# Row maxima of causal attention from the exponentials' operands, on the whole array, in three buffers

## What is computed

```python
scores = jnp.einsum('bhqd,bhkd->bhqk', q, k) * D ** (-0.5)
scores = jnp.where(causal, scores, -jnp.inf)
weights = jax.nn.softmax(scores, axis=-1)     # needs each query's maximum first
out = jnp.einsum('bhqk,bhkd->bhqd', weights, v)
```

## Time and profile before

| | |
|---|---|
| runs | 719.22 us median (716.24, 719.22, 719.84) |
| the profiled execution's own time | 713.31 us |
| its span, first to last instruction | 711.5 us |
| mean granted TensorE clock | 0.949 of full speed |
| TensorE (PE) busy | 616.2 us, 87% |
| VectorE (DVE) busy | 504.4 us, 71% |
| ScalarE (ACT) busy | 455.0 us, 64% |
| GpSimd (POOL) busy | 259.0 us, 36% |
| DMA | 52.09 MB in 33323 packets |

### The profile page before, as it was taken

One profiled execution on the slowest core, in us unless ns is written; L12 is line 12 of the kernel. 1 busy time (PEld: TensorE's weight loads), 2 busy tenths in 40 slices (PEclk: granted clock), 3 DMA queues, 4 the chain that ended last, 5 costly groups with the idle time before them and its releaser, 6 DMA issues.

```text
span 711.5 us, 14086 instructions
## 1 busy us (share of the span) xinstructions
PE 616.2 (87%) x4988; PEld 293.0 (41%) x5052; DVE 504.4 (71%) x825; ACT 455.0 (64%) x908; POOL 259.0 (36%) x459
## 2 busy tenths in 40 slices
PE   0687399499988999999999999899999999999983
PEld 0455033245453555444352354432333333346632
DVE  7967588375775546888978978599988898843222
ACT  0463156266646688778766676687777777766781
POOL 5665021314300211687111106791132221116883
PEclk9788579799998999999999999999999999999997
DMA  5057431300551300306230444063331330200002
GB/s 175 0 180 156 125 121 40 68 1 31 139 156 41 71 28 4 95 23 189 75 91 18 81 116 126 2 180 125 71 85 33 80 67 18 53 2 1 1 0 60
DMA packets 33323, 52.09 MB, mean 73 GB/s; under 512 B 5832, under 2 KB 23912, under 8 KB 30696
## 3 DMA queue, kind: packets, MB, share of 16 engines
q1 hardware_dynamic: 31960, 50.74, 26.8%
q10 hardware_dynamic: 1296, 0.46, 0.2%
HBM read 37.29 MB, written 13.63 MB: 72 GB/s over the span
## 4 chain that ended last, share of the span: by engine, by line
PE 56%; DVE 13%; POOL 12%; ACT 6%; issue 6%; DMA 4%; SPq 2%; another core or an unknown queue 0%; POOLq 0%; ACTq 0%; DVEq 0%
PE ps L1319 52%; DVE maxes L1302 5%; ACT probs L1034 3%; DVE sine L1156 2%; POOL gate L550 2%; DMA qop<-shiftT 2%; SPq L736 2%; POOL probs L862 2%; PE ps L1534 1%; DMA F<-in_w 1%; POOL xn L550 1%; PE ps L1373 1%; POOL gate L907 1%; POOL gate L908 1%; POOL x L897 1%
## 5 line engine op out<-in xcount | busy, mean ns | idle before, releaser
L1302 DVE TENSOR_REDUCE maxes<-ps 128x2 f32<-128x1024 f32 (+2 forms) x288 | 338.6, 1220 | 91.1 <-PE ps L1319 89.5
L1034 ACT ACTIVATE probs<-ps 128x512 f32<-128x512 f32 x576 | 305.3, 605 | 110.0 <-PE ps L1319 68.5
L1319 PE MATMUL ps<-qop,kop 128*128 128x512 bf16 (+3 forms) x704 | 163.8, 327 | 22.4 <-DMA qop<-shiftT 9.3
L862 POOL TENSOR_SCALAR_AFFINE_SELECT probs<-probs 128x512 f32<-128x512 f32 (+1 forms) x160 | 83.8, 546 | 249.1 <-ACT probs L1034 249.1
L1319 PE MATMUL ps<-probs,vals 128*9 128x512 f32 (+3 forms) x1536 | 150.1, 493 | 4.9 <-POOL probs L862 3.1
L1319 PE MATMUL ps<-kmx,qmx 32*128 32x128 bf16 (+2 forms) x1280 | 101.9, 269 | 20.6 <-DMA qop<-shiftH 8.9
L1319 PEld LDWEIGHTS ps<-qop,kop 128*128 128x128 bf16 x768 | 60.2, 99 | 110.7 <-ACT probs L1034 50.0
L1319 PEld LDWEIGHTS ps<-kmx,qmx 32*128 32x128 bf16 x1280 | 38.1, 93 | 118.4 <-issue 66.4
L1319 PE MATMUL ps<-F 128*128 128x128 f32 (+2 forms) x640 | 76.9, 283 | 5.4 <-DMA F<-in_w 3.9
L1319 PEld LDWEIGHTS ps<-F 128*128 128x128 f32 (+2 forms) x640 | 69.2, 181 | 20.2 <-issue 16.3
L1319 PEld LDWEIGHTS ps<-probs,vals 128*9 128x9 f32 x1536 | 29.7, 90 | 60.5 <-issue 43.8
(11 more groups left out here) (158 smaller groups left out, 643.4 us busy)
## 6 DMA issues: line engine op xcount, KB each, us to landing
qop<-q_thirds SPq DMA_DIRECT2D x48, 192.0 KB
kop<-k_thirds SPq DMA_DIRECT2D x48, 192.0 KB
qmx<-q_thirds SPq DMA_DIRECT2D x16, 256.0 KB
kmx<-k_thirds SPq DMA_DIRECT2D x16, 256.0 KB
F<-in_w SPq DMA_DIRECT2D x16, 256.0 KB, 5.1
q_thirds<-third SPq DMA_DIRECT2D x8, 384.0 KB, 4.4
k_thirds<-third SPq DMA_DIRECT2D x8, 384.0 KB, 3.8
q_thirds<-third SPq DMA_DIRECT2D x8, 256.0 KB, 3.3
```

Source lines behind the costliest of these rows:

```text
L862: last = pool.affine_select(where, where, [[0, number], [1, P]], ALU.is_ge, 0.0, base=0, channel_multiplier=-1)
L1034: act.activation(probs[:, u % RING, :], bank(at), ACT.Exp, scale=SCALE).then_inc(s_cells_read, 1)
L1302: dve.tensor_reduce(dst, src, AX.X, ALU.max).then_inc(s_units_read[pair // 2], 1)
L1319: return pe.matmul(out_, lhsT, rhs, start=first, stop=last)
```

## The change

The operands for the maxima, their loads and the DRAM planes that only they used are gone. A max product now reads rows 0 to 125 of `qop` and `kop`, the whole height of the array, one head after the other. The shift's rows move to 126 and 127. `qop` and `kop` get three buffers, so a load waits for the group three back. For groups 0 and 8 the load comes in two halves, each after its own half of the store, with its own semaphore; their max units are cut so that the first six need only half 0 (20 units instead of 18). The shift's DMAs are issued by ACT, right behind its copy, not by SP. The planner gets new costs and a new `MORE` table, and no longer counts max units as a tiling of their own.

```diff
-KR = TERMS * D
+KR = P - 2
-QUERY_COPIES = ((0, 0, 2), (2, 0, 3))
-KEY_COPIES = ((0, 0, 3), (3, 0, 2), (5, 1, 1), (6, 0, 1))
+QUERY_COPIES = ((0, 0, 3),)
+KEY_COPIES = ((0, 0, 3), (3, 0, 2))
+DEEP = 3
...
+HALVES = [[(2, 0, 256), (3, 0, 256)], DIAGONALS[0], [(1, 0, 128), (3, 256, 128)], [(5, 512, 128), (7, 768, 128)]] + LATER_ROWS
...
-SHAPE = {"max": "rows", "pv": "columns", "eo": "halves"}
-STAY = {"whole": 27.0, "rows": 57.0, "columns": 20.0, "halves": 10.0, None: 0.0}
+SHAPE = {"pv": "columns", "eo": "halves"}
+STAY = {"whole": 2.0, "rows": 160.0, "columns": 29.0, "halves": 10.0, None: 0.0}
...
 MORE = {
-    "add": (47, -2), "attT": (-5, -48), "colsum": 13, "comb": 49, "count": -1, "ct": 2, "diag": -80, "disp": 17, "emb": 4,
...
+    "add": (160, 45), "attT": (55, -88), "colsum": 157, "comb": -18, "count": 160, "ct": -11, "diag": 118, "disp": -120,
...
-        masks = 2 * COLUMN * BANK + TILING + 0.1 if arg[1] // 2 in DIAGONAL else 0.0
-        return COLUMN * BANK + masks, "D", (("DVE", 1.2),)
+        pieces = pattern(arg[0])[arg[1] // 2]
+        masks = 2 * COLUMN * BANK if pieces in DIAGONALS else 0.0
+        return 2 * COLUMN * sum(w for _, _, w in pieces) + masks, "D", (("DVE", 0.1 + 0.0022 * sum(w for _, _, w in pieces)),)
...
     if kind == "ldexp":
-        return [("ldmax", n)] + ([("exp", n - 2, NU - 1)] if n >= 2 else [])
+        return [("store", n // NG, 2 * (n // GB % 2) + half) for half in ((0, 1) if c == 2 else (c,))] + (
+            [("exp", n - DEEP, NU - 1)] if n >= DEEP else [])
...
-        qmx = sb("qmx", [P, 2, T], BF16)
-        kmx = sb("kmx", [P, 2, T], BF16)
-        qop = sb("qop", [P, 2, HG, T], BF16)
-        kop = sb("kop", [P, 2, HG, T], BF16)
+        qop = sb("qop", [P, DEEP, HG, T], BF16)
+        kop = sb("kop", [P, DEEP, HG, T], BF16)
...
-                elif kind == "ldmax":
...
+                elif kind == "ldexp":
+                    n, part = arg
+                    r, L, b, heads = n % DEEP, n // NG, n // GB % 2, slice(n % GB * HG, n % GB * HG + HG)
+                    for half in (0, 1) if part == 2 else (part,):
                         sp.wait_ge(s_stored[half], STORES * (2 * L + b + 1))
+                    if n >= DEEP:
+                        sp.wait_ge(s_cells_full, CELL["exp", n - DEEP, NU - 1] + 1)
...
+                        sp.dma_start(qop[rows_i, r, :, some], q_rows).then_inc(s_loaded[0 if part == 2 else part][r], 16)
+                        sp.dma_start(kop[rows_i, r, :, some], k_rows[D * i:D * i + 3 * D]
+                                     ).then_inc(s_loaded[1 if part == 2 else part][r], 16)
-                elif kind == "shift":
-                    n, part = arg
-                    sp.wait_ge(s_cells_read, CELL[what] + 1)
...
@@ ACT, shift
+                        act.wait_ge(s_cells_read, CELL[what] + 1)
+                        for k in range(2):
+                            act.dma_start(qop[KR + k:KR + k + 1, r, :, :], shiftT[HG * TB * k:HG * TB * k + HG * TB, :]
+                                          ).then_inc(s_shift_in[k][r], 16)
...
@@ PE, max
-                    pe.wait_ge(s_mload[r], 32 * (n // 2 + 1))
+                    for half in (0, 1) if n not in SPLIT or u >= units(n, 0) else (0,):
+                        pe.wait_ge(s_loaded[half][r], 48 * arrivals(n))
...
-                            rows_h = slice(MR * h, MR * h + MR)
-                            last = mm(bank(pair + k)[:, c:c + w], qmx[rows_h, r, P * i:P * i + P],
-                                      kmx[rows_h, r, k0:k0 + w], not diagonal, not diagonal or c + w == BANK)
+                            last = mm(bank(pair + k)[:, c:c + w], qop[0:KR, r, h, P * i:P * i + P],
+                                      kop[0:KR, r, h, k0:k0 + w], not diagonal, not diagonal or c + w == BANK)
```

More of the change, by code:

```diff
@@ L101, in parts, with pattern, units, arrivals @@
     return (0, 1) if n in SPLIT else (2,)
+def pattern(n):
+    return HALVES if n in SPLIT else PATTERN
+def units(n, part=2):
+    return 6 if part == 0 else 2 * len(pattern(n))
+def arrivals(n):
+    return n // DEEP + 1 + sum(k <= n and k % DEEP == n % DEEP for k in SPLIT)
 def of_part(kind, n, part):
@@ L131 @@
 WINDOW, KEEP, REGAIN = 3.4133, 0.48, 0.8
-WEIGHT = {"max": 0.25, "shift": 0.25}
+WEIGHT = {"shift": 0.25}
 ENGINES = ("PE", "ACT", "DVE", "POOL", "SP")
+OF_GROUPS = ("max", "exp", "pv", "top", "shift", "halve", "pvout", "out", "mask", "ldmax", "ldexp")
 MORE = {
-    "add": (47, -2), "attT": (-5, -48), "colsum": 13, "comb": 49, "count": -1, "ct": 2, "diag": -80, "disp": 17, "emb": 4,
[L137 to L144, removed]
@@ new lines @@
+    "add": (160, 45), "attT": (55, -88), "colsum": 157, "comb": -18, "count": 160, "ct": -11, "diag": 118, "disp": -120,
+    "emb": -119, "embT": 58, "embstat": 5, "eo": 158, "es": -35, "exp": (48, -75), "halve": (-99, -77), "heads": (-45, 129),
+    "hid": 48, "hid1": -104, "high": (-102, 103, -120), "ldexp": (138, 28), "ldf1": -82, "ldw": -11, "ldwA": -31,
+    "ldwB": 110, "left": (-51, 75, -50), "lg": -28, "limit": 93, "ln": 122, "lnroot": 12, "lnstat": 56, "logit": -17,
+    "low": (-27, -38, 130), "lt": 145, "mask": (106, 150), "max": (33, -61), "middle": (142, -37, 26), "mix": -85,
@@ new lines @@
+    "norm": (16, 131, -3), "offs": -40, "out": (37, -45), "proj": (-31, -98), "pv": (-94, -114), "pvout": (76, 134),
+    "qk": (54, 133, 65), "rT": 151, "rden": (-99, -97), "res": -120, "root": (-120, 48), "routes": 20, "rs": 45,
+    "shift": (-77, -45), "silu": (137, -21), "slot": 76, "soft": 96, "stat": (-120, -47, -117), "store": (-103, -45, -98),
+    "sum": (125, 13, 119), "top": (24, -24), "total": -62, "v": (145, 16, 30), "wg": 116, "xT": (-78, 63, 155), "xr": -93,
+    "xrT": 5, "z": -102,
@@ L145 @@
 }
-OF_GROUPS = ("max", "exp", "pv", "top", "shift", "halve", "pvout", "out", "mask", "ldmax", "ldexp")
 LATER = {"lt": "soft", "lg": "comb"}
@@ L300, in needs @@
         return [("lnroot", L)]
[L301 to L303 removed]
     if kind == "ldexp":
[L305 removed]
+        return [("store", n // NG, 2 * (n // GB % 2) + half) for half in ((0, 1) if c == 2 else (c,))] + (
+            [("exp", n - DEEP, NU - 1)] if n >= DEEP else [])
     if kind == "max":
[L307 removed]
+        return [("ldexp", n, parts(n)[u >= units(n, parts(n)[0])])] + ([("top", n - 1, parts(n - 1)[-1])] if n and u == 0 else [])
     if kind == "top":
[L309 removed]
+        return [("max", n, units(n, c) - 1)] + (of_part("halve", n - 2, c) if n >= 2 else [])
     if kind == "halve":
@@ L324, in needs @@
         return [("mask", n, u) if STEP[u][4] else ("exp", n, STEP[u][0] + STEP[u][1] - 1)] + (
-            [("v", n // NG, 2 * (n // GB % 2) + k) for k in range(2)] if u == 0 else []) + (
+            [("v", n // NG, 2 * (n // GB % 2) + STEP[u][2])] if start else []) + (
             [("pvout", n, 0) if u else ("pvout", n - 1, 1)] if start and (n or u) else [])
@@ L348, in more @@
     if isinstance(extra, tuple):
-        extra = extra[what[1] // NG if what[0] in OF_GROUPS else what[1]]
+        if len(extra) == 3:
+            extra = extra[2] if what[1] else extra[what[2] // 2]
+        else:
+            extra = extra[what[1] // NG if what[0] in OF_GROUPS else what[1]]
     return extra
@@ L383, in streams @@
     groups = range(2 * NG)
-    made += [[("ldmax", n) for n in groups], [("ldexp", n) for n in groups]]
-    made.append([("max", n, u) for n in groups for u in range(NM)])
+    made += [[(kind, n, part) for n in groups for part in parts(n)] for kind in ("ldexp",)]
+    made.append([("max", n, u) for n in groups for u in range(units(n))])
     made += [[(kind, n, part) for n in groups for part in parts(n)] for kind in ("top", "halve", "shift")]
@@ L753, in _ @@
                     else:
                         sp.wait_ge(s_ones, 2)
-                    q_rows = q_dram[L][b, 2:5, :, heads, :].rearrange("a d h t -> (a d) (h t)")
-                    k_rows = k_dram[L][b, 0:5, :, heads, :].rearrange("a d h t -> (a d) (h t)")
+                    some = slice(0, T) if part == 2 else slice(BANK * part, BANK * part + BANK)
+                    q_rows = q_dram[L][b, :, :, heads, some].rearrange("a d h t -> (a d) h t")
+                    k_rows = k_dram[L][b, :, :, heads, some].rearrange("a d h t -> (a d) h t")
@@ L1304, in _ @@
                     n, part = arg
-                    done = UNITS_DONE[part]
-                    for u in (done - 2, done - 1):
+                    for u in range(units(n, part) - 2, units(n, part)):
                         last = UNIT["max", n, u]
```

102 lines of the change are left out of this document (40 added, 62 removed), and 1 row of the table COST.

## The result

The changed kernel takes 724.54 us (median of 5 runs, 723.36 to 725.84) beside 718.43 us for the kernel before on the same chip: a ratio of 1.0114, 95% interval 1.0084 to 1.0143, slower by some 8 us. The forecast was 712 us, faster. The number lies inside the range, the sign is the wrong one. All times and ratios here are of executions at the usual clock; two others, of 943.5 us (experiment 4) and 991.1 us (experiment 7) at a granted clock of 0.66 and 0.56, are left out.

What follows compares the result with a forecast made beforehand. Transfers were taken to set the early stretch (28 to 140 us), PE the middle (140 to 650 us). Terms -26 + 25 + 4 - 3 - 7 = -7 us took 719.2 to 712 us, range 696 to 731.

Steps and rivals of the forecast that it cites:

- The unit's price: Maximum products on PE: a whole-array max unit takes 0.44 us, with changes of stationary operand every 128 columns hidden.
- The sum of the products: All maximum products on PE: whole-height products cost +25 us, bounds +12 (two thirds absorbed in waits) and +37 (none).
- ACT issues the shifts: 32 shift DMAs on ACT hold it 19 us, exponentials queueing behind: taken +4 us, bounds 0 and +19.
- Early part: Stretch from 28 to 140 us: earlier first load and faster shifts gain 26 of 28.6 us, bounds -10 and -35.
- (a): First load, early stretch: loading by halves lets it go out at 42 us and PE start 9 us earlier.
- (c): Group 1's shift, early stretch: three buffers and another queue cut its landing from 11.9 to 1.9 us, saving 10.0 us.
- (b): First shift, early stretch: issued by ACT at once and landing in 1.9 us, it saves 9.6 us.
- Clock, -3: PE's granted clock: fewer stretches at the lower level early and from 215 to 231 us, -3 us, bounds 0 and -5.
- Order, -7: Planner's new order: fewer tiling switches around `pv` and a shorter tail save 7 us, bounds -18 and +8.
- the early gain is small because ACT's queue lands in 8.5 us: Rival, early stretch: DVE's pace or ACT's 8.5 us landing leaves -13 instead of -26, 725 us; chance 0.10.
- ACT is late: Rival, every group: exponentials stand 1.3 us behind the shift, +15 instead of +4, 723 us; chance 0.08.
- PE pays in full: Rival, middle stretch: lost side-by-side products cost the whole +37 us, 731 us, or 728 with better order; chance 0.22.

Runs made afterwards that it cites:

- experiment 4: The changed kernel, shifts still issued by ACT, but SP waits at the shift's place until the shift has landed: 714.53 us, ratio 0.9959 to the kernel before.
- experiment 7: The kernel before with the changed kernel's table of due times and likings, nothing else: 733.51 us, ratio 1.0224 to the kernel before.
- experiment 3: The changed kernel with the shifts' DMAs back on SP, at their place in SP's order: 707.92 us, ratio 0.9882 to the kernel before.
- experiment 8: The changed kernel with shifts on SP, groups 0 and 8 loading their first half only after both halves are stored: 711.52 us, ratio 0.992 to the kernel before.
- experiment 2: The kernel before, only the shifts' DMAs issued by ACT behind its copy instead of by SP: 722.17 us, ratio 1.0072 to the kernel before.
- experiment 5: The changed kernel, ACT issuing shifts, SP waiting until each has landed, run again for a profile: 714.39 us, ratio 0.9971 to the kernel before.

## Why the prediction was wrong, point by point

- **Which part is bound by what.** Right. PE's idle time from 28 to 140 us fell from 34 to 13 us (forecast: some 15), the middle stayed PE's at 95% busy. (Some of the 26 idle us of the middle are products that the trace lacks; with all of them in the trace, experiment 3's middle is 98% busy.)
- **The unit's price**, 0.44 us, and no cost for changing weights every 128 columns: right (0.43 and 0.44). **The sum of the products**, +25 with bounds +12 and +37: 20 us alone in the old order, half of a known amount in the new one. Nearly right in size. The reason given, "part of it falls into waits" for DVE, isn't shown: PE's own waits for DVE fell by 2.9 us. The +37 for no absorption was too high, and that the +25 came out near is in part luck.
- **The step that failed: "ACT issues the shifts. Taken +4; bounds 0 and +19."** It costs some 17 us. Of these at most 6, more likely some 3, are ACT being held by the issue, 1.2 us a group, so that part was sized about right. The 11 us that SP's wait gives back I had in the text as a question, and answered wrongly: "How fast ACT's queue lands a shift ... I take 1.9". It landed a shift in up to 8.0 us beside six loads, and in 6.8, 6.1 and 7.8 us in the chain. The nearer row was the 8.5 us of ACT's queue at the start, which I had put down as the other end. I also priced that case only where SP's stall had been, not where the removal of SP's stop creates a new one: in SP's order the shift stood *ahead* of the next loads, and SP waited for it there. That place in the order looked like a cost and was what kept the next loads from running beside the shift. "The loads ... only relieve SP" was the sentence that hid it. A row was misread on the way: the six loads ahead of group 1's shift in the kernel before were not "its own group's" but group 2's, the next one's (groups 0 and 1 were loaded from 54 to 61 us). That row already showed what a shift meets when the next loads go first.
- **The Trainium skill's rule.** The Trainium skill says that a DMA engine goes round its queues packet by packet (DMA: Bandwidth & Descriptors, "Queues, rings and completion order"). The trace agrees as far as it can tell: at 188 us the shift's packets pass among SP's and end before them. What I drew from it, that the 26 us were safe, the runs don't bear out: with SP's loads in flight ACT's 8 KB took 6.8 to 10.6 us in the two chains shown, without them 1.9. A turn among the queues does not mean a prompt landing, when beside it packets of 8 KB take 0.6 us each.
- **Early part, (a) to (c), -26.** (a), 9 us for the first load, is some 3 us by experiment 8: the load went out at 47.3, not 42, and the first maxima came 17 us after it, not earlier than before. (b) and (c) rested on 1.9 us, and on ACT's queue they fail: alone they bring group 1's copy 3.2 us forward and make the kernel 5 us slower. With the shifts on SP and the new order the stalls of the early part are gone; one landing of 6.1 us, at 217 us, is left.
- **Clock, -3.** Right in direction: 0.949 to 0.967, and over 0.97 with SP's wait (0.974) or the shifts on SP (0.980). The stalls cost clock as well: after the one at 191 us the clock was 0.50 from 195 to 198 us.
- **Order, -7.** Not shown. I argued with fewer runs of `pv`; in the order that the planner writes there are 144 instead of 127. The last stretch did not shrink by itself.
- **The sum.** Without ACT's share the forecast was -11 us; the version without it measures -8.5. Of the rivals, "the early gain is small because ACT's queue lands in 8.5 us" (725 us) named the cause, but for the early part, where PE's idle time fell as forecast; the slow landings came in the middle. "ACT is late" (723 us) came true in part. That both stand within 2 us of the measured time is luck: neither says what happened. "PE pays in full", with 0.22 the one I feared, did not come true.

## What to carry to other kernels

A wait in a queue's order can be doing work: before a small, urgent transfer is moved to another queue, see what its old queue will issue in its place. Keep such a transfer ahead of the large ones on the same queue, or hold them until it has landed; here holding them is worth 11 of 717 us, and leaving the issuing to SP another 6, not all of it ACT's time. Read the chain for slow landings, as the summary line of a tile can lack them. And when a change brings a new schedule, test its parts with the schedule held fixed, as a table tuned for one kernel cost 16 to 46 us on the other.

## What was not expected of the hardware

An 8 KB transfer on ACT's queue beside six loads of 192 KB on SP's took 6.8 us (at 188 us, changed kernel) and 10.6 us (at 122 us, experiment 2) to land, against 1.9 us alone, although nothing else was on its own queue: its 96 packets passed among SP's packets of 8 KB, in 4.7 us (at 188 us) instead of 0.8. And what a DMA issue costs the engine behind it is the whole of it: 1.16 us for two, after which the exponential that was ready started 1.57 us after the copy instead of 0.32. Over thirteen such steps experiment 5 fell only 1.6 us further behind.
